# Four transformer layers on one core: the first attention's small matmuls on other array tiles and PSUM banks, and part of the first gated unit on GpSimd

## The chip, the cores and the metric

One core of a Trainium2 chip runs the whole program. The metric is the device time of one execution in microseconds (us), as the median of several runs. TensorE (PE in the profile) multiplies matrices, VectorE (DVE), ScalarE (ACT) and GpSimd (POOL) work elementwise, SyncE (SP) issues most DMAs. Matmuls write to PSUM, which has 8 banks of 512 fp32 columns by 128 partitions.

## The reference, cut to what matters

The input `x` is 16 sequences of 64 rows with 512 columns, handled as 8 row tiles of 128 rows. The program runs four layers of cross attention and feed-forward network. Only the first layer is touched:

```
x = x + attention0(layernorm(x), ctx)     # windows of 16 queries, 32 keys, 8 heads in the 64-row axis
x = x + ffn0(layernorm(x))
# ffn0:
xs = bf16(x); qg, sg = quant(xs * inv_gate); qu, su = quant(xs * inv_up)     # integers up to 127, a scale per row
gate = qg @ w_gate.T * sg * s_wgate
up   = qu @ w_up.T   * su * s_wup
inter = bf16(clip(silu(gate) * up, -10, 10))
qi, si = quant(inter * inv_inter)
out = qi @ w_down.T * si * s_wdown
```

Layers 1 to 3 follow (the second attention with 32 heads of 128 is by far the longest) and are the same code before and after.

## The kernel before, in words

Each engine has its own instruction stream, written in the order of one common list, `ORDER`, which `stage_order` makes; every entry is a stage name and an index. An engine runs its stream in order and waits on semaphores. A stage's PSUM bank comes from `psum_uses`; `psum_table` counts how often each bank is filled, and whoever fills a bank next waits until the last reader has freed it. A bank that two kinds of stage share is therefore handed over in the order of the list.

The first attention is worked in 32 groups `u`, four per row tile. The stages of a group, several steps of the list apart, are:

- `l0_qk` (once in four groups): the projections q and k; ScalarE spreads them out of banks 4 and 7 (L1774, L1780).
- `l0_project` (L795): the values. 16 matmuls with 64 contraction rows, 32 stationary and 128 moving columns. An fp32 matmul shows as two instructions in the trace.
- `l0_scores` (L813 the band mask, L817 the products): four array tiles of 32 by 32, 8 products of 64 columns on each; one bank, 0 and 1 in turn. VectorE takes the maximum and subtracts it (L1372, L1377; the latter frees the bank), ScalarE exponentiates.
- `l0_sum` (L1381, L1384) on VectorE, then GpSimd multiplies (L2158).
- `l0_turn` (L828) transposes, `l0_weigh` (L844) weights the values, `l0_out` (L859) projects into bank 6; VectorE adds that to `X` and frees bank 6 (L1392).

The first ffn of a row tile is interleaved, a stage every half step: layer norm; `f0_quant` and `f0_quant_u` (VectorE L1294 to L1298, ScalarE L1817); the transposes `f0_turn` (bank 7) and `f0_turn_u` (both L750), copied by ScalarE to `qgT`, `quT` (L1836); `f0_gate` on TensorE (L880, L882) and VectorE (L1417, L1418); the exponential on ScalarE (L1850); `f0_silu`; `f0_quant2`; `f0_turn2`; `f0_down` (L896 to L900, bank 6), read by VectorE at L1443. `f0_turn_u` stands in the list directly behind the `l0_weigh` that follows `f0_turn`, so that on TensorE the order there is `f0_turn`, `l0_out`, `l0_weigh`, `f0_turn_u`, `l0_turn`, `f0_gate`. For row tiles 0 to 5 it fills bank 0.

Four groups make one period, which also carries one row tile of ffn. Below its groups are called A, B, C, D: A follows `f0_down`, B holds the two transposes and `f0_gate`, C holds `l0_qk` and `f0_silu`, D holds `f0_quant2`, `f0_turn2` and ends with the next `f0_down`.

Of the kernel before, what the change touches and what calls it, by code (L numbers as in the profile page):

```python
# [17 lines left out]
NT = 8  # L18
# [215 lines left out]
def psum_uses(stage, i):  # L234
# [7 lines left out]
    if stage == "l0_scores":  # L242
        return [("S", (0, 1))]
# [8 lines left out]
    if stage == "f0_turn_u":  # L252
        return [("u", (0 if i < NT - 2 else 3 if i < NT - 1 else 6,))]
# [144 lines left out]
def build_program(nc, d, out):  # L398
    ctx = ExitStack()
    with ctx:  # L400
# [51 lines left out]
        def bank(use):  # L452
            return banks[use.bank // 2][:, 512 * (use.bank % 2):512 * (use.bank % 2) + 512]

# [275 lines left out]
        def tensor_program(pe):  # L730
# [50 lines left out]
            def l0_project(u):  # L781
                t, g = divmod(u, 4)
                cn, d_cn, n_cn = cn_place(t)
                on.wait_ge(D.w0, 16)
                on.wait_ge(D.pad, 16)
                p = PSUM["l0_project", u, "v"]
                on.wait_ge(d_cn, n_cn)
                on.wait_ge(S.zero, 2)
                on.wait_ge(p.free, p.n)
                for k in range(4):  # L790
# [12 lines left out]
            def l0_scores(u):  # L803
                t, g = divmod(u, 4)
                p, q, k = PSUM["l0_scores", u, "S"], PSUM["l0_qk", 4 * t, "q"], PSUM["l0_qk", 4 * t, "k"]
# [4 lines left out]
                pairs = [slice(32 * h, 32 * h + 32) for h in range(4)]  # L810
# [20 lines left out]
            def l0_weigh(u):  # L831
# [8 lines left out]
                for j in range(4):  # L840
                    for p, r in zip((p0, p1), halves):
                        for h in range(4):
                            c = j * 128 + 32 * h
# [59 lines left out]
            def l1_q(i):  # L903
                h, t = divmod(i, NT)
                p = PSUM["l1_q", i, "p"]
                lt_ready("l1", t)
                on.wait_ge(p.free, p.n)
# [83 lines left out]
            def l1_d(i):  # L991
                n = weight_turn(i)
                if n is not None:
                    on.wait_ge(S.mx4, n + 1)
                    on.wait_ge(S.zero, 9)
# [255 lines left out]
        def vector_program(v):  # L1251
# [92 lines left out]
            def begin(_):  # L1344
# [6 lines left out]
                v.memset(mgp, MAGIC).then_inc(S.zero, 1)  # L1351

# [15 lines left out]
            def l0_scores(u):  # L1368
                p = PSUM["l0_scores", u, "S"]
                s3, p3 = [x.rearrange("p (g k) -> p g k", k=32) for x in (em[u % 3], bank(p))]  # L1370
                on.wait_ge(p.full, p.n + 1)
                on.mark(v.tensor_reduce(mx0[u % 2], p3, AX, MAX))  # L1372
# [4 lines left out]
                v.tensor_tensor(s3, p3, bc(mx0[u % 2], 32), SUB).then_inc(p.free, 1)  # L1377
# [31 lines left out]
            def f0_gate(t):  # L1409
# [3 lines left out]
                on.wait_ge(S.sx, t)  # L1413
                if t:
# [5 lines left out]
            def f0_silu(t):  # L1420
                p = PSUM["f0_gate", t, "p"]
# [697 lines left out]
        def pool_program(g):  # L2119
# [54 lines left out]

            def f0_silu(t):
                on.wait_ge(S.it, t + 1)
                if t:
# [103 lines left out]
            def f3_mm(t):  # L2281
# [8 lines left out]
                      f0_silu=f0_silu, f0_down=f0_down, l1_k=l1_k, l1_z=l1_z, f1_quant=f1_quant, l2_begin=l2_begin, l2_a=l2_a, l2_z=l2_z, f2_split=f2_split,  # L2290
# [8 lines left out]
        def sync_program(s):  # L2299
# [14 lines left out]
            def begin(_):  # L2314
# [12 lines left out]
                for c in range(4):  # L2327
                    for k in range(2):
                        load(view(cT, c * 2048 + 192 * k, [[256, 8], [1, 64]]), d["cT"][:, c, k], D.ct)
                load(wq1, d["w1"][0][:, 0:2048], D.wq1)  # L2330
                load(w1, d["w1"][0][:, 2048:3072], D.kv1)

            def l0_norm(u):
# [7 lines left out]
                load_cn(t + 1)  # L2341

# [148 lines left out]
def host_layout(i):  # L2491
# [15 lines left out]
    order = np.arange(128).reshape(2, 8, 8).transpose(1, 0, 2).reshape(128)  # L2507
    p = np.arange(128)
    bq, bk, bv, bo = [np.tile(i[f"L0_xattn_b{n}"], 2)[:, None] for n in "qkvo"]
    pairs = (p[:, None] // 16 % 2 == np.arange(2)[None, :]).astype(np.float32)  # L2510
    own = (p[:, None] // 8 % 2 == np.arange(2)[None, :]).astype(np.float32)
# [74 lines left out]
```

## Time and profile before

| | us |
|---|---|
| median of 3 runs | 1567.65 (1567.29 to 1570.88) |
| profiled execution, its own time | 1568.3 |
| its span, first to last instruction | 1566.5 |
| TensorE busy | 1489.1 (95%) |
| VectorE busy | 819.6 (52%) |
| ScalarE busy | 748.8 (48%) |
| GpSimd busy | 439.2 (28%) |

The granted TensorE clock averaged 0.988 of full speed. Shares over the whole span are means over stages with different limits; the first layer is the first 240 us or so. Times in the trace are counted from the start of the span.

### The profile page before, as it was taken

How to read it: one execution, taken by the hardware profiler on the slowest of the kernel's cores; microseconds unless marked ns; L12 is line 12 of the kernel's file. 1: busy time of each engine (PE TensorE's matmuls, PEld its weight loads, DVE VectorE, ACT ScalarE, POOL GpSimd, SP SyncE). 2: the span in 40 equal slices, each digit the busy share in tenths (PEclk: the TensorE clock that was granted, in tenths of full speed). 3: DMA queues.
4: the chain of work that ended last, by engine and by line, in shares of the span. 5: the costliest groups of instructions: out<-in, count | busy, mean ns of one | idle time of the engine just before them, and what ended most of it. 6: DMA issues, size and time to landing. Idle time of an engine off the chain costs nothing. (4 is left out here: it accounts for less than half of the span.)

```text
span 1566.5 us, 32999 instructions
## 1 busy us (share of the span) xinstructions
PE 1489.1 (95%) x13154; PEld 1228.5 (78%) x13154; DVE 819.6 (52%) x1681; ACT 748.8 (48%) x2560; POOL 439.2 (28%) x557
## 2 busy tenths in 40 slices
PE   6988979999999999999999999879999999999998
PEld 4767768888989888888989887556656778888876
DVE  3678875544444555544443447766665421343465
ACT  4565545454545445454544565355443312455552
POOL 1355343222222212222222224255221000123333
PEclk8999999999999999999999999899999999999999
DMA  8000010020100101010010110020100001122111
GB/s 252 13 17 10 10 44 28 28 75 28 41 28 3 40 27 41 28 41 28 4 38 28 41 55 1 2 83 1 41 1 1 26 6 56 48 74 74 47 27 62
DMA packets 44537, 58.62 MB, mean 37 GB/s; under 512 B 25520, under 2 KB 32704, under 8 KB 41568
## 3 DMA queue, kind: packets, MB, share of 16 engines
q1 hardware_dynamic: 43872, 56.05, 11.4%
q8 instruction: 104, 1.70, 0.5%
q10 hardware_dynamic: 448, 0.46, 0.1%
q14 instruction: 49, 0.40, 0.1%
q0 software_dynamic: 64, 0.00, 0.0%
HBM read 48.89 MB, written 2.10 MB: 33 GB/s over the span
## 5 line engine op out<-in xcount | busy, mean ns | idle before, releaser
L1872 ACT ACTIVATE big<-pb 128x128 f32<-128x128 f32 x384 | 106.5, 277 | 300.9 <-PE pb L912 198.2
L2211 POOL TENSOR_TENSOR big<-big 128x512 f32<-128x512 f32 x96 | 99.9, 1040 | 260.4 <-DVE big L1503 260.4
L1921 ACT ACTIVATE big<-pb,big 128x128 f32<-128x128 f32 x384 | 135.7, 367 | 58.0 <-issue 34.2
L1498 DVE TENSOR_REDUCE big<-pb 128x4 f32<-128x512 f32 x96 | 65.8, 686 | 178.1 <-PE pb L951 170.5
L927 PE MATMUL pb<-wkh,CXh 128*128 128x256 f32 x512 | 150.0, 293 | 0.0
L927 PE MATMUL pb<-wkl,CXh 128*128 128x256 f32 x512 | 145.4, 284 | 0.0
L927 PE MATMUL pb<-wkh,CXl 128*128 128x256 f32 x512 | 144.6, 282 | 0.0
L2201 POOL TENSOR_SCALAR big<-big 128x6 f32<-128x6 f32 x64 | 12.8, 199 | 413.1 <-ACT big L1872 412.5
L1290 DVE TENSOR_TENSOR X<-X,pb 128x512 f32<-128x512 f32 x128 | 86.9, 679 | 74.8 <-PE pb L1138 39.3
L978 PE MATMUL pb<-woh,oh 128*128 128x512 f32 x256 | 114.3, 446 | 0.0
L912 PE MATMUL pb<-wqh,CXh 128*128 128x512 f32 x256 | 101.9, 398 | 3.0 <-DVE big L1468 1.5
L978 PE MATMUL pb<-woh,ol 128*128 128x512 f32 x256 | 103.1, 403 | 0.0
L978 PE MATMUL pb<-wol,oh 128*128 128x512 f32 x256 | 102.0, 399 | 0.0
L912 PE MATMUL pb<-wqh,CXl 128*128 128x512 f32 x256 | 101.3, 396 | 0.0
L912 PE MATMUL pb<-wql,CXh 128*128 128x512 f32 x256 | 101.2, 395 | 0.0
L966 PE MATMUL pb<-big 128*128 128x256 f32 (+1 forms) x384 | 98.8, 380 | 0.1
L927 PEld LDWEIGHTS pb<-wkh,CXl 128*128 128x128 f32 x512 | 97.8, 191 | 0.0
L927 PEld LDWEIGHTS pb<-wkh,CXh 128*128 128x128 f32 x512 | 97.5, 190 | 0.0
L927 PEld LDWEIGHTS pb<-wkl,CXh 128*128 128x128 f32 x512 | 97.4, 190 | 0.0
L1488 DVE COPY big<-pb 128x512 f32<-128x512 f32 x56 | 38.7, 690 | 101.5 <-PE pb L939 101.0
L2128 POOL TENSOR_SCALAR ve<-mv 128x1 f32<-128x1 f32 x64 | 14.3, 224 | 274.7 <-DVE mv L1272 272.6
L2206 POOL TENSOR_TENSOR big<-big,half 128x6 f32<-128x6 f32 x64 | 84.7, 1324 | 9.4
(279 smaller groups left out, 3790.7 us busy)
## 6 DMA issues: line engine op xcount, KB each, us to landing
big<-in_w SPq DMA_DIRECT2D x17, 1024.0 KB, 5.0
big<-in_w SPq DMA_DIRECT2D x24, 256.0 KB, 3.0
big<-in_w SPq DMA_DIRECT2D x8, 512.0 KB, 3.6
o<-o SPq DMA_DIRECT2D x96, 32.0 KB, 1.9
X<-in_x SPq DMA_DIRECT2D x8, 256.0 KB, 5.4
big<-in_cn SPq DMA_DIRECT2D x8, 256.0 KB, 2.8
CXlf<-in_cT SPq DMA_DIRECT2D x8, 256.0 KB, 5.9
big<-in_wa SPq DMA_DIRECT2D x1, 2048.0 KB, 7.6
```

Of the source, the lines that this page charges most:

```text
L912: a = pe.matmul(bank(p), x_rows(x, c, t), y[:, 512 * c:512 * c + 512], start=(n == 0), stop=(n == 11))
L927: a = pe.matmul(bank(p)[:, s * 256:s * 256 + 256], kv_rows(x, c, 2 * t + s), y[:, 256 * c:256 * c + 256], start=(n == 0), stop=(n == 11), ...
L966: a = pe.matmul(bank(p)[0:hd, s * 256:s * 256 + 256], v_of(s), pt[:, s * 256:s * 256 + 256], start=(s == 0), stop=True, skip_group_check=True)
L978: a = pe.matmul(bank(p), x[:, 128 * c:128 * c + 128], y[:, 512 * c:512 * c + 512], start=(n == 0), stop=(n == 3 * size - 1))
L1290: v.tensor_tensor(X[:, t, :], X[:, t, :], bank(p), ADD).then_inc(p.free, 1)
L1488: v.tensor_copy(QT[i % 2].rearrange("p (b h q) -> p h b q", b=2, h=4), bank(p).rearrange("p (h b q) -> p h b q", h=4, b=2)).then_inc(p.fre ...
L1498: v.tensor_reduce(m[j % 2], quarters(bank(p)), AX, MAX, negate=True).then_inc(S.m, 1)
L1872: y = a.activation(sq[i % 2], bank(p)[:, j * width:j * width + 128], ACT.Square, accum_out=ss[i % 2][:, first + j:first + j + 1])
L1921: y = a.activation(e_[:, c], bank(p)[:, c], ACT.Exp, bias=m[j % 2][:, k:k + 1], scale=1.0, accum_out=z[j % 2][:, k:k + 1])
L2128: g.tensor_scalar(ve[:, n % 4, :], mv[:, n % 4, 1:2], 1e-5, None, ADD).then_inc(*on.to(S.pool))
L2206: g.tensor_tensor(rr[i % 2][:, 0:6], ss[i % 2][:, 0:6], half[:, 0:6], ALU.pow).then_inc(*on.to(S.rr))
L2211: g.tensor_tensor(quarters(e_), quarters(e_), bc(r[j % 2], 128), MUL).then_inc(*on.to(S.pn))
```

## The change: tiles, banks, one silu on GpSimd, and later loads

- Values: 64 moving columns in place of 128 per matmul (head channels are laid out so that each batch half needs only its own 64); the other half of the bank is zeroed once, by VectorE, at the start.
- Scores: eight array tiles instead of four, row group h with column groups h and h+2; the first 256 columns of bank 0 and of bank 1 together hold one group. There is one such buffer, so the next group's scores wait until this group's are subtracted.
- `f0_turn_u` of row tiles 0 to 5 goes to bank 6 in place of bank 0.
- `f0_silu`: VectorE keeps the addition of 1 and the reciprocal; GpSimd makes gate times up (early), the product with the reciprocal, and the clamp.
- DMAs of `cT` (8) and of layer 1's weights (2) leave the start of SP's queue and stand behind its loads of `cn` for row tiles 2 and 3.

```diff
     if stage == "l0_scores":
-        return [("S", (0, 1))]
+        return [("S", (1,))]
...
     if stage == "f0_turn_u":
-        return [("u", (0 if i < NT - 2 else 3 if i < NT - 1 else 6,))]
+        return [("u", (6 if i < NT - 2 else 3 if i < NT - 1 else 6,))]
...
-                            a = pe.matmul(bank(p)[key, k * 128:k * 128 + 128], cn[rows_, at:at + 32], wv0[rows_],
-                                          start=(k == 0), stop=True, skip_group_check=True)
+                            a = pe.matmul(view(bank(p)[key], k * 128 + 16 * b, [[32, 4], [1, 16]]), cn[rows_, at:at + 32],
+                                          view(wv0[rows_], 16 * b, [[32, 4], [1, 16]]), start=(k == 0), stop=True,
+                                          skip_group_check=True)
...
-                for r in pairs:
+                tiles = [(e, slice(32 * h, 32 * h + 32), slice((32 * h + 64 * e) % 128, (32 * h + 64 * e) % 128 + 32))
+                         for e in range(2) for h in range(4)]
+                for e, r, c in tiles:
                     b = bandb[r.start:r.start + 16]
-                    pe.matmul(bank(p)[r], b[:, 0:32], b[:, 128:640], start=True, stop=False, skip_group_check=True)
-                for i in range(8):
-                    n = 8 * g + i
-                    for r in pairs:
-                        a = pe.matmul(bank(p)[r, i * 64:i * 64 + 64], Qx[t % 2][r, n * 32:n * 32 + 32],
+                    pe.matmul(two_banks[c, e, 0:256], b[:, 0:32], b[:, 128:384], start=True, stop=False, skip_group_check=True)
+                for i in range(4):
+                    for e, r, c in tiles:
+                        n = 8 * g + 4 * e + i
+                        a = pe.matmul(two_banks[c, e, i * 64:i * 64 + 64], Qx[t % 2][r, n * 32:n * 32 + 32],
...
+                v.memset(bank(PSUM["l0_project", 0, "v"]), 0.0).then_inc(S.zero, 1)
...
                 on.mark(v.tensor_scalar(e0, e0, 1.0, None, ADD))
                 on.wait_ge(S.dve, on.n)
-                on.mark(v.reciprocal(e0, e0))
-                on.wait_ge(S.dve, on.n)
-                on.mark(v.tensor_tensor(e0, e0, g0, MUL))
-                on.wait_ge(S.dve, on.n)
-                on.wait_ge(p.free, p.n + 1)
-                on.mark(v.tensor_tensor(e0, e0, u0, MUL))
-                on.wait_ge(S.dve, on.n)
-                on.wait_ge(S.mi, t)
-                v.tensor_scalar(it0, e0, -10.0, 10.0, MAX, MIN).then_inc(S.it, 1)
+                v.reciprocal(e0, e0).then_inc(S.it, 1)
...
+            def f0_gate(t):
+                p = PSUM["f0_gate", t, "p"]
+                on.wait_ge(S.sg, t + 1)
+                on.wait_ge(p.free, p.n + 1)
+                on.wait_ge(*on.last)
+                g.tensor_tensor(u0, u0, g0, MUL).then_inc(*on.to(S.pool))
+
             def f0_silu(t):
                 on.wait_ge(S.it, t + 1)
+                on.wait_ge(*on.last)
+                g.tensor_tensor(e0, e0, u0, MUL).then_inc(*on.to(S.pool))
+                on.wait_ge(*on.last)
+                g.tensor_scalar(it0, e0, -10.0, 10.0, MAX, MIN).then_inc(*on.to(S.pool))
...
-                for c in range(4):
-                    for k in range(2):
-                        load(view(cT, c * 2048 + 192 * k, [[256, 8], [1, 64]]), d["cT"][:, c, k], D.ct)
-                load(wq1, d["w1"][0][:, 0:2048], D.wq1)
-                load(w1, d["w1"][0][:, 2048:3072], D.kv1)
...
                 load_cn(t + 1)
+                if t == 1:
+                    for c in range(4):
+                        for k in range(2):
+                            load(view(cT, c * 2048 + 192 * k, [[256, 8], [1, 64]]), d["cT"][:, c, k], D.ct)
+                if t == 2:
+                    load(wq1, d["w1"][0][:, 0:2048], D.wq1)
+                    load(w1, d["w1"][0][:, 2048:3072], D.kv1)
```

The order of the stages is the same. TensorE's stream in a group B, before (pb3 holds banks 6 and 7, pb0 banks 0 and 1; a wait on `bank6_free` is for VectorE's L1392):

```order
L795 MATMUL pb1<-big 32x128 x15
L750 MATMUL pb3<-ident,big 128x128 [waits f0_q_gate]
L750 MATMUL pb3<-ident,big 128x128 x3
L859 MATMUL pb3<-big 128x128 [waits bank6_free,bank5_free,bank4_free]
L859 MATMUL pb3<-big 128x128
L844 MATMUL pb2<-big 32x32 [waits bank3_free]
L844 MATMUL pb2<-big 32x32 x31
L750 MATMUL pb0<-ident,big 128x128 [waits bank0_free,f0_q_up]
L750 MATMUL pb0<-ident,big 128x128 x3
L828 MATMUL pb1<-ident,big 128x128 [waits l0_probs]
```

The same place after the change (its line numbers are a few higher: L752 for L750, L866 for L859, L835 for L828):

```order
L798 MATMUL pb1<-big 32x4x16 x15
L752 MATMUL pb3<-ident,big 128x128 [waits f0_q_gate]
L752 MATMUL pb3<-ident,big 128x128 x3
L866 MATMUL pb3<-big 128x128 [waits bank6_free,bank5_free,bank4_free]
L866 MATMUL pb3<-big 128x128
L851 MATMUL pb2<-big 32x32 [waits bank3_free]
L851 MATMUL pb2<-big 32x32 x31
L752 MATMUL pb3<-ident,big 128x128 [waits bank6_free,f0_q_up]
L752 MATMUL pb3<-ident,big 128x128 x3
L835 MATMUL pb1<-ident,big 128x128 [waits l0_probs]
```

No row has moved; the second transpose waits for bank 6, which the `l0_out` two rows above it fills, where it waited for bank 0.

VectorE's stream in the same group B after the change, from the layer norm statistics of the next row tile to the read of that `l0_out`; it is the same sequence as before:

```order
L1385 TENSOR_REDUCE big<-pb0 128x16 [waits bank1_full]
L1390 TENSOR_TENSOR big<-pb0,big 128x512 [waits dve_step,bank3_full]
L1278 BN_STATS st<-X 128x6 [waits d_row4]
L1282 BN_AGGR mv<-st 128x2 [waits dve_step,ln_rows]
L1296 TENSOR_SCALAR xn<-X,mv,rs 128x512 [waits bank4_full,ln_rstd]
L1405 SCALAR_TENSOR_TENSOR X<-pb3,big,X 128x128 [waits bank6_full]
```

L1405 (L1392 before) is what frees bank 6, and it stands behind the group's own scores, the statistics and the normalized rows.

## Rows read from the trace of the kernel before

**Rows 1.** Windows: stretch, length, busy PE, PEld, DVE, ACT, POOL (instructions), clock, DMA share, GB/s.
```profile
0.00:88.26 88.26, 70.53 (x2017) 52.33 (x2018) 46.72 (x106) 46.75 (x93) 22.14 (x35) 0.94 0.41 120
88.26:197.42 109.16, 97.87 (x2930) 77.79 (x2930) 86.91 (x188) 64.29 (x135) 54.98 (x64) 1.00 0.04 11
144.22:170.82 26.60, 23.99 (x733) 19.31 (x732) 21.57 (x47) 15.10 (x32) 11.41 (x15) 1.00 0.05 14
197.42:243.18 45.76, 36.55 (x900) 31.28 (x899) 31.66 (x67) 22.11 (x56) 16.92 (x19) 0.93 0.12 38
243.18:1566.50 1323.32, 1284.13 (x7314) 1067.08 (x7312) 654.33 (x1320) 615.63 (x2276) 345.15 (x440) 0.99 0.11 34
```

**Rows 2.** Timeline of TensorE, one period: start, duration, engine, line, instruction, idle before.
```profile
144.22 0.39 PE L813 MATMUL pb<-big 16*32 16x512 bf16 x4
144.44 1.06 PE L817 MATMUL pb<-big 32*32 32x64 f32 x64
145.44 1.08 PE L795 MATMUL pb<-big 64*32 64x128 f32 x32
146.44 0.71 PE L859 MATMUL pb<-big 128*128 128x128 f32 x4
...
148.36 0.39 PE L813 MATMUL pb<-big 16*32 16x512 bf16 x4
...
150.59 0.66 PE L750 MATMUL pb<-ident,big 128*128 128x128 f32 x4
...
151.62 0.76 PE L844 MATMUL pb<-big 64*32 64x32 f32 x64
...
152.79 0.65 PE L750 MATMUL pb<-ident,big 128*128 128x128 f32 x4 [0.42 <-ACT big L1817]
...
155.05 0.39 PE L880 MATMUL pb<-CXh,qgT 128*128 128x256 f32 x1 [1.17 <-ACT qgT L1836]
...
157.57 0.40 PE L813 MATMUL pb<-big 16*32 16x512 bf16 x4
```

**Rows 3.** Timeline of ScalarE, VectorE and GpSimd in that period.
```profile
144.33 0.75 DVE L1443 SCALAR_TENSOR_TENSOR big<-pb,big 128x512 f32<-128x512 f32 x1 [1.17 <-PE pb L900]
...
149.13 0.82 ACT L1817 ACTIVATE big<-big 128x512 f32<-128x512 f32 x1 [0.92 <-DVE big L1298]
...
155.60 0.35 DVE L1392 SCALAR_TENSOR_TENSOR X<-pb,big,X 128x128 f32<-128x128 f32 x1
...
158.69 0.69 DVE L1310 TENSOR_TENSOR CXl<-pb,CXh 128x512 fp32r<-128x512 f32 x1 [0.56 <-ACT CXh L1721]
...
159.29 0.68 DVE L1372 TENSOR_REDUCE big<-pb 128x16 f32<-128x512 f32 x1
...
161.01 1.75 DVE L1425 RECIPROCAL big<-big 128x256 f32<-128x256 f32 x1
...
162.79 0.42 DVE L1427 TENSOR_TENSOR big<-big 128x256 f32<-128x256 f32 x1
...
163.71 0.29 DVE L1433 TENSOR_SCALAR big<-big 128x256 bf16<-128x256 f32 x1
...
164.09 0.68 POOL L2181 TENSOR_TENSOR big<-big 128x256 f32<-128x256 bf16 x1 [6.13 <-DVE big L1433]
...
165.07 0.36 DVE L1294 TENSOR_REDUCE big<-big 128x1 f32<-128x256 f32 x1
...
165.23 1.05 POOL L2158 TENSOR_TENSOR big<-big 128x512 f32<-128x512 f32 x1 [0.47 <-DVE big L1384]
```

**Rows 4.** Windows around two stretches in which TensorE stood still, columns as in Rows 1.
```profile
30.74:33.92 3.18, 0.00 (x1) 0.00 (x0) 0.00 (x0) 0.14 (x1) 0.00 (x0) 0.98 0.60 131
33.92:40.40 6.48, 6.48 (x123) 4.72 (x127) 3.55 (x7) 3.00 (x7) 0.00 (x0) 0.50 0.80 286
231.10:233.88 2.78, 0.01 (x2) 0.03 (x1) 1.32 (x6) 1.27 (x4) 2.30 (x4) 1.00 0.85 330
233.88:238.80 4.92, 4.92 (x29) 4.92 (x30) 1.41 (x4) 3.09 (x11) 0.00 (x0) 0.65 0.03 10
```

More of the change, by code:

```diff
@@ L453, in bank @@
             return banks[use.bank // 2][:, 512 * (use.bank % 2):512 * (use.bank % 2) + 512]
+        two_banks = banks[0].rearrange("p (e n) -> p e n", e=2)
         X = sb("X", [128, NT, 512])
@@ L789, in l0_project @@
                 on.wait_ge(p.free, p.n)
+                on.wait_ge(S.zero, 9)
                 for k in range(4):
@@ L804, in l0_scores @@
                 t, g = divmod(u, 4)
-                p, q, k = PSUM["l0_scores", u, "S"], PSUM["l0_qk", 4 * t, "q"], PSUM["l0_qk", 4 * t, "k"]
+                q, k = PSUM["l0_qk", 4 * t, "q"], PSUM["l0_qk", 4 * t, "k"]
+                p = PSUM["l0_scores", u, "S"]
                 on.wait_ge(q.free, q.n + 1)
@@ L842, in l0_weigh @@
                         for h in range(4):
-                            c = j * 128 + 32 * h
+                            c = j * 128 + 32 * ((h + j // 2 * 2) % 4)
                             a = pe.matmul(bank(p)[32 * h:32 * h + 32, j * 32:j * 32 + 32],
@@ L906, in l1_q @@
                 lt_ready("l1", t)
+                if i == 0:
+                    scores = PSUM["l0_scores", 4 * NT - 1, "S"]
+                    on.wait_ge(scores.free, scores.n + 1)
                 on.wait_ge(p.free, p.n)
@@ L994, in l1_d @@
                     on.wait_ge(S.mx4, n + 1)
-                    on.wait_ge(S.zero, 9)
+                    on.wait_ge(S.zero, 10)
                     turn_b(PSUM["l1_d", i, "w4"], q4[n % 2])
@@ L1369, in l0_scores @@
                 p = PSUM["l0_scores", u, "S"]
-                s3, p3 = [x.rearrange("p (g k) -> p g k", k=32) for x in (em[u % 3], bank(p))]
+                s4 = em[u % 3].rearrange("p (e g k) -> p e g k", e=2, k=32)
+                p4 = two_banks[:, :, 0:256].rearrange("p e (g k) -> p e g k", k=32)
+                m3 = mx0[u % 2].rearrange("p (e g) -> p e g", e=2)
                 on.wait_ge(p.full, p.n + 1)
-                on.mark(v.tensor_reduce(mx0[u % 2], p3, AX, MAX))
+                on.mark(v.tensor_reduce(m3, p4, AX, MAX))
                 if u >= 3:
@@ L1376, in l0_scores @@
                 on.wait_ge(S.dve, on.n)
-                v.tensor_tensor(s3, p3, bc(mx0[u % 2], 32), SUB).then_inc(p.free, 1)
+                v.tensor_tensor(s4, p4, m3.unsqueeze(3).broadcast_to([128, 2, 8, 32]), SUB).then_inc(p.free, 1)
             def l0_sum(u):
@@ L1413, in f0_gate @@
                 on.wait_ge(S.sx, t)
+                on.wait_ge(S.mi, t)
                 if t:
@@ L1420, in f0_silu @@
             def f0_silu(t):
-                p = PSUM["f0_gate", t, "p"]
                 on.wait_ge(S.sx, t + 1)
@@ L2289, in pool_program @@
             do = dict(begin=begin, l0_bias=l0_bias, l0_norm=l0_norm, l0_sum=l0_sum, l0_ctx=l0_ctx, f0_norm=f0_norm,
-                      f0_silu=f0_silu, f0_down=f0_down, l1_k=l1_k, l1_z=l1_z, f1_quant=f1_quant, l2_begin=l2_begin, l2_a=l2_a, l2_z=l2_z, f2_split=f2_split,
+                      f0_gate=f0_gate, f0_silu=f0_silu, f0_down=f0_down, l1_k=l1_k, l1_z=l1_z, f1_quant=f1_quant, l2_begin=l2_begin, l2_a=l2_a, l2_z=l2_z, f2_split=f2_split,
                       l3_z=l3_z, l3_c=l3_c, f3_mm=f3_mm)
@@ L2505, in diag @@
         return z
-    order = np.arange(128).reshape(2, 8, 8).transpose(1, 0, 2).reshape(128)
+    order = np.arange(128).reshape(2, 4, 16).transpose(1, 0, 2).reshape(128)
     p = np.arange(128)
     bq, bk, bv, bo = [np.tile(i[f"L0_xattn_b{n}"], 2)[:, None] for n in "qkvo"]
-    pairs = (p[:, None] // 16 % 2 == np.arange(2)[None, :]).astype(np.float32)
-    own = (p[:, None] // 8 % 2 == np.arange(2)[None, :]).astype(np.float32)
+    pairs = (p[:, None] // 8 % 2 == np.arange(2)[None, :]).astype(np.float32)
+    own = (p[:, None] // 16 % 2 == np.arange(2)[None, :]).astype(np.float32)
     m["w0"] = np.concatenate([diag(i["L0_xattn_Wq"].T)[:, order], diag(i["L0_xattn_Wk"].T)[:, order],
```

1 line of the change is left out of this document (removed).

## The prediction, made before the changed kernel ran

> **What bounds the kernel now.** I read the busy shares first: TensorE is busy 95% of the span. That is a mean, and the change touches only the first layer, so I read the windows by stage next [rows 1]. From 243 us on the stream is as before, and TensorE is busy 1284 of 1323 us there, so whatever shift stands at 243 us stands at the end. In the first layer one period of four groups lasts 26.60 us, with TensorE busy 23.99 and VectorE 21.57 [rows 1]: TensorE leads, VectorE is close behind. Third came the timelines of that period, to see which engine each wait ends on [rows 2, 3]. VectorE starts L1443 at 144.33, right behind the down projection, and from there to the end of L1392 at 155.95 it is never free for long: 11.62 us of work in a row, the GpSimd steps of two layer norms included [rows 3]. TensorE does not wait for that L1392 before; it only matters that the bank is free a group later.
>
> **The matmuls.** In a group, scores take 144.22 to 145.44, or 1.22 us, values 145.44 to 146.44, or 1.00 us [rows 2]. The scores' 64 instructions of 64 columns on four tiles run at 1.06/64 = 16.6 ns each. The value matmuls also occupy only four different tiles (two row halves, two column groups for each) and now have 64 columns, so I price them like the scores: 32 x 16.6 ns = 0.53 us, a gain of 0.47. Bounds: 32 instructions at the 11.9 ns of L844 (0.76/64, eight tiles [rows 2]) give 0.38; no gain gives 1.00. Scores on eight tiles: from 64 x 11.9 ns = 0.76 less what the modelled end adds, to the present 1.06 us; I take 0.69, as L844 is the only row with eight tiles and its successor starts sooner than its end. The masks (0.22 us) I leave as they are. Together 0.84 us less per group, 32 groups, or 27 us, if TensorE were always the bound.
>
> The Trainium skill, page "TensorE: Matmul & The Clock Gate", section "Part 1: The HAM clock gate", says that the start-to-start distance of matmuls never falls under about 25 ns, however few columns they have. L844's 64 instructions in 0.76 us [rows 2] contradict it for tiled matmuls, and so do the scores. By the page the values would gain 0.2 us per group instead of 0.47 and the scores nothing; the first 88 us would then give back about 4 us less.
>
> **The wait that is added.** In group B the second ffn transpose (L750 at 152.79) now needs bank 6, which the l0_out just before it has filled and which only VectorE's L1392 frees. In this period that ends at 155.95 [rows 3]. I place everything from the end of the down projection, 144.22. TensorE's new arrival: group A's 4.14 us less 0.84, scores and values of B 1.22 + 1.00 - 0.84, that is 148.90; it waits for ScalarE's L1817 (149.13 + 0.82) until 150.0; transpose, l0_out, l0_weigh as in 150.59 to about 152.3, so it stands at the transpose at 151.7. VectorE's 11.62 us have not become shorter: nothing in them waits for TensorE, and none of their instructions is removed. So TensorE idles from 151.7 to 156.0, 4.3 us, where it lost 0.42 before. Behind the transpose in its queue are l0_turn, the gate matmuls, and group C. Transpose and l0_turn take 1.1 us, so the gate starts at 157.1 where it started at 155.05 (before, it waited 1.17 us for ScalarE's quantized rows [rows 2], which are now ready early): 2.0 us late.
>
> From there to the next down projection the chain doesn't run over TensorE's scores. VectorE's L1372 of group C starts behind L1310 at 159.29 [rows 3], after the scores are done; then the reciprocal, sum, quant2, scores of D, ScalarE's copy of the quantized rows, transpose, down projection. It took 170.82 - 157.57 = 13.25 us. The silu part: before, the reciprocal ends at 162.76, two products and the clamp go on to 163.92, GpSimd's product (0.68) ends at 164.77, 2.0 us in all. Now GpSimd does product, clamp, product. I take 0.65 for a 256-column fp32 product (between VectorE's 0.42 and the 0.68 of L2181, whose one operand is bf16; half of L2158's 1.05 is 0.53), 0.5 for the clamp (between VectorE's 0.29 and 0.68), 0.68, and 0.2 of handing over: 2.0 us again. VectorE sheds 1.13 us per row tile there, but l0_out's addition and l0_sum take only 1.15, and then quant2 (L1294) waits for GpSimd about 0.9 us: it starts 2.3 us behind the reciprocal, at 165.05, against 165.07. So the 9 us taken from VectorE over eight row tiles buy at most 0.2 per period. Bounds: clamp and product at 0.4 together gain 0.2 (then group D's scores on TensorE are last), at 1.6 they cost 0.5.
>
> Sum of a period at full clock: 11.7 to the freed bank, 3.7 to group C's scores (transpose and l0_turn 1.1, gate and l1_turn 2.5), 13.0 from there: 28.4 us against 26.6. The four periods of 88.26:197.42 took 109.16 us, two of them longer through casts and instruction stalls that partly hide in the new idle; new 4 x 28.4 + 0.5 = 114.1, so +4.9. A fifth such wait follows in 197.42:243.18 (row tile 5; tiles 6 and 7 keep their banks); I take it like the others, 1.8, less 0.3 for its faster scores: +1.5.
>
> **The clock.** Where TensorE stood still for 3.18 us, the granted clock was 0.50 for the next 6.48 us; after 2.78 us it was 0.65 over 4.92 us [rows 4]. 0.50 and below-one means are time at the lower of its two levels, 1.2 GHz. Losses: 6.48 x 0.50 = 3.2 us and 4.92 x 0.35 = 1.7 us. After the 1.17 us before L880 it stayed at full speed. The new stillness of 4.3 us is longer than both, and what follows it (gate, l1_turn, scores of C) is on the path. I charge 2.0 us each, five times: +10. Bounds 0 and 3.2 each.
>
> **The first 88 us.** Nine groups have no wait on bank 6. Light groups gain the full 0.84. Those with l0_qk gain only about 0.4, because l0_weigh then waits for ScalarE's spreading of q, which starts from VectorE's subtraction. Groups around the first gate gain little, since VectorE leads. Added up: u0 0.6, u1 0.3, u2 0.4, u3 1.3 (it runs at half clock), u4 and u5 0.85 each, u6 0.2, u7 0.85, u8 0.4, u10 and u11 0.5 together: 6.3 us. The single score buffer costs nothing where VectorE is ready: its two reads take at most 1.72 us (159.29 to 161.01 [rows 3]), while TensorE has 148.36 - 145.44 - 0.47 = 2.45 us of other work between two scores [rows 2]. The moved loads: TensorE stood still 3.18 us at 30.74 while DMA was 60% busy [rows 4]; cT is now issued from about 25 on, so the same collision can come again. I count 1 us for them, bounds 0 and 6 (stall and clock gone).
>
> **Sum.** -6.3 - 1 + 4.9 + 1.5 + 10 = +9.1, on the profiled execution: span 1575.6, own time 1577.4 with the 1.8 us around it. The median of the runs lay 0.65 below that execution: 1576.8, say 1577.
>
> **Rivals.**
> - The clock doesn't fall, or what it costs is hidden behind VectorE: +9.1 - 10 = -0.9, 1567. For it: much of C waits on ScalarE anyway. Against it: two stretches in the trace, both shorter. Chance 0.17; within 0.3%.
> - The long fall: 3.2 us each and GpSimd at its upper bound, +6 and +2.5: 1585. Chance 0.15.
> - Faster: the loads decide. The stall at 30.74 and its slow stretch go (-5 more), tiles reach their lower bounds (-2), and the clock's price is 1 us each or less (-5): 9.1 - 12 = -3, 1565; it decides once the clock costs under 1.2 us each and the stall is gone. If in addition VectorE's chain up to L1392 shortens by 2 us, so that the wait is hidden (it would need another engine's step in it to go, and I see none), the five waits vanish: 1552. Chance together 0.15, of which 0.12 faster by over 0.3%.
>
> My forecast has 0.53. Changes within 0.3% (4.7 us) can't be told from none here. Slower by more: the forecast and the long fall, nearly all, 0.67; within: 0.20; faster: 0.13. Range: 1564 to 1586.
>
> **What would show it.** In the new profile: the second transpose of five groups B with about 4 us idle before it, released by VectorE's read of l0_out; a granted clock of 0.5 to 0.7 behind each; periods of 29 to 31 us; value matmuls of 0.5 us per 32; L1294's 256-column form with an idle of 0.5 to 1 us ended by GpSimd; VectorE's idle before the gate up by 2 us. Wrong would be: periods under 27 us, which means VectorE reaches that L1392 sooner than 11.6 us after the down projection; no idle before the transpose; value matmuls still 1 us.

## The result, and the profile after

The median of the changed kernel is 1591.66 us (4 runs, 1587.02 to 1592.70), that of the kernel before in the same job 1567.47 (4 runs, 1563.49 to 1570.88). The ratio is 1.015, 95% interval 1.0118 to 1.0181: slower by 24 us, where +9 was forecast. The direction was right, the time lies outside the range. The profiled execution took 1592.56 us against 1568.3, so the traces differ by the same 24 us. They are compared stage by stage below; each is one execution, and a stage of one execution can be off by several us, as shown further down. One of the six executions of e11 (below) was a slow run, 1865.71 us at a granted clock of 0.743, and neither its ratio nor its median in the table uses it.

The page of the changed kernel: span, busy time and share of each engine, and the granted clock in 40 slices of about 40 us.
```profile
span 1590.5 us, 33255 instructions
PE 1478.3 (93%) x13282; PEld 1223.0 (77%) x13282; DVE 810.6 (51%) x1658; ACT 750.1 (47%) x2560; POOL 460.9 (29%) x581
PEclk7899879999999999999999999999999999999999
```
TensorE is busy 11 us less than before and the kernel takes 24 us more, so its waiting grew by 35. The matmuls alone are about 24 us shorter at full clock (0.75 us in each of 32 groups, below); the busy time fell by less than half of that, because more of it ran at the low clock. The low digits stand in the first seven slices, the first layer.

Windows of the changed kernel, cut at the same places of the program as [rows 1] (scores of groups 12, 20, 28, and the same matmul of the second attention's stream at 268.57):
```profile
0.00:91.45 91.45, 65.02 (x2064) 48.79 (x2065) 46.04 (x104) 46.94 (x93) 24.76 (x38) 0.85 0.40 116
91.45:218.42 126.97, 96.49 (x2993) 79.63 (x2992) 81.64 (x176) 64.85 (x135) 65.30 (x76) 0.88 0.03 10
122.78:153.95 31.17, 23.48 (x749) 19.34 (x748) 20.45 (x44) 16.87 (x35) 18.71 (x21) 0.89 0.04 12
218.42:268.57 50.15, 34.56 (x915) 30.04 (x915) 30.58 (x64) 22.03 (x56) 19.51 (x22) 0.86 0.11 34
268.57:1590.50 1321.93, 1282.25 (x7314) 1064.52 (x7312) 652.32 (x1314) 616.33 (x2276) 351.35 (x446) 0.99 0.11 34
```
Against [rows 1]:

| stretch | before | after | difference | in the prediction |
|---|---|---|---|---|
| up to group 12 | 88.26 | 91.45 | +3.2 | -7.3 |
| four periods | 109.16 | 126.97 | +17.8 | +12.9 (4.9 and four clock falls) |
| to the common point | 45.76 | 50.15 | +4.4 | +3.5 (1.5 and a fifth fall) |
| the rest | 1323.32 | 1321.93 | -1.4 | 0 |
| sum | | | +24.0 | +9.1 |

TensorE in one period after, to be laid beside [rows 2]:
```profile
122.91 0.84 PE L824 MATMUL pb<-big 32*32 32x64 f32 x64
123.67 0.65 PE L798 MATMUL pb<-big 64*32 64x64 f32 x32
124.25 0.71 PE L866 MATMUL pb<-big 128*128 128x128 f32 x4
...
130.25 0.76 PE L851 MATMUL pb<-big 64*32 64x32 f32 x64
134.85 1.09 PE L752 MATMUL pb<-ident,big 128*128 128x128 f32 x4 [3.84 <-DVE X L1405]
135.73 1.06 PE L835 MATMUL pb<-ident,big 128*128 128x128 f32 x4
136.44 0.56 PE L887 MATMUL pb<-CXh,qgT 128*128 128x256 f32 x1
136.80 0.42 PE L889 MATMUL pb<-wgl,qgT 128*128 128x256 f32 x1
...
140.38 0.30 PE L820 MATMUL pb<-big 16*32 16x256 bf16 x8
...
153.95 0.30 PE L820 MATMUL pb<-big 16*32 16x256 bf16 x8
```
From start to start the scores take 0.76 us (1.00 before), the values 0.58 (1.00 before), the masks 0.13 (0.22 before): 0.75 us less per group, where the prediction had 0.84. Then the second transpose stands 3.84 us for VectorE's L1405, the read that frees bank 6, and what follows runs slowly: behind the first pair, the gate's matmuls (L887 and L889 in turn) start 0.21 us apart, where at full speed they start 0.12 apart. The windows of that place, with the clock in the third column from the right:
```profile
131.01:134.85 3.84, 0.00 (x1) 0.03 (x1) 2.64 (x7) 3.00 (x7) 1.75 (x3) 0.74 0.01 4
134.85:140.47 5.62, 5.62 (x36) 5.46 (x44) 1.12 (x4) 1.27 (x2) 2.33 (x2) 0.57 0.00 0
140.47:153.95 13.48, 10.70 (x368) 8.06 (x366) 9.30 (x20) 9.00 (x19) 7.39 (x9) 1.00 0.08 24
```
The clock falls within this standstill already (0.74 over it). 5.62 us at a mean clock of 0.57 (86% of it at 1.2 GHz) are 5.62 x 0.43 = 2.4 us lost, on the path to group C.

This happens six times, once for each row tile 0 to 5: the waits at the second transpose are 1.03, 3.85, 3.84, 2.70, 4.11 and 5.44 us, and the clocks from there to the next group's masks 0.62, 0.53, 0.57, 0.65, 0.55 and 0.63. Worked out the same way, an estimate, the six slow stretches lose 12.9 us together.

VectorE and GpSimd in that period, beside [rows 3]:
```profile
122.89 0.75 DVE L1448 SCALAR_TENSOR_TENSOR big<-pb,big 128x512 f32<-128x512 f32 x1 [1.45 <-PE pb L907]
...
134.36 0.34 DVE L1405 SCALAR_TENSOR_TENSOR X<-pb,big,X 128x128 f32<-128x128 f32 x1
...
140.05 0.48 DVE L1431 SCALAR_TENSOR_TENSOR big<-pb,big 128x256 f32<-128x256 f32 x1 [4.47 <-PE pb L889]
...
145.65 0.73 POOL L2190 TENSOR_TENSOR big<-big 128x256 f32<-128x256 f32 x1 [3.85 <-DVE big L1438]
146.46 1.08 POOL L2192 TENSOR_SCALAR big<-big 128x256 bf16<-128x256 f32 x1
147.69 0.68 POOL L2197 TENSOR_TENSOR big<-big 128x256 f32<-128x256 bf16 x1
...
148.41 0.42 DVE L1304 TENSOR_REDUCE big<-big 128x1 f32<-128x256 f32 x1 [1.78 <-POOL big L2197]
```
From L1448 to the end of L1405 are 11.8 us (11.6 before): VectorE's chain is what it was, and TensorE, which now comes to it earlier, waits for it. VectorE in turn waits 4.47 us for the gate, where it waited 0.41 before:
```profile
157.24 0.48 DVE L1417 SCALAR_TENSOR_TENSOR big<-pb,big 128x256 f32<-128x256 f32 x1 [0.41 <-PE pb L882]
```
GpSimd's clamp takes 1.08 us.

### The profile page after: what moved, and what is told of

Same layout as the page of the kernel before. It is cut to its first block and busy times, and to the rows that moved or that the text cites. A ratio compares the mean times of both kernels' runs of the same rounds, so it can differ in the third digit from the quotient of the medians.

```text
span 1590.5 us, 33255 instructions
## 1 busy us (share of the span) xinstructions
PE 1478.3 (93%) x13282; PEld 1223.0 (77%) x13282; DVE 810.6 (51%) x1658; ACT 750.1 (47%) x2560; POOL 460.9 (29%) x581
## 5 line engine op out<-in xcount | busy, mean ns | idle before, releaser
L1503 DVE TENSOR_REDUCE big<-pb 128x4 f32<-128x512 f32 x96 | 65.9, 686 | 178.6 <-PE pb L961 170.2
L2217 POOL TENSOR_SCALAR big<-big 128x6 f32<-128x6 f32 x64 | 12.9, 202 | 410.4 <-ACT big L1877 409.7
```

Source lines behind the costliest of these rows:

```text
L1503: v.tensor_reduce(m[j % 2], quarters(bank(p)), AX, MAX, negate=True).then_inc(S.m, 1)
```

## The experiments

Fifteen kernels ran. The ratio is always to the kernel before on the same chip; 0.1% is 1.6 us. "us" is ratio less one, times 1568. Differences between two rows carry both intervals; they are given below as plus or minus so many us.

| kernel | median | ratio (95%) | us |
|---|---|---|---|
| e1 before, transpose in bank 6 | 1584.08 | 1.0092 (1.0071 to 1.0114) | +14.4 |
| e2 after, transpose in bank 2 | 1576.46 | 1.0059 (1.0039 to 1.0079) | +9.3 |
| e3 after, the wait filled | 1580.70 | 1.0073 (1.0048 to 1.0099) | +11.4 |
| e4 before, values alone | 1570.55 | 1.0004 (0.9988 to 1.0020) | +0.6 |
| e5 before, GpSimd silu alone | 1570.43 | 1.0020 (1.0010 to 1.0031) | +3.1 |
| e6 after, silu on VectorE | 1589.37 | 1.0141 (1.0121 to 1.0161) | +22.1 |
| e7 after, `l0_rows` later | 1579.50 | 1.0083 (1.0053 to 1.0113) | +13.0 |
| e8 before, `l0_rows` later | 1568.95 | 1.0009 (0.9996 to 1.0022) | +1.4 |
| e9 before, moved loads alone | 1568.76 | 1.0007 (0.9996 to 1.0018) | +1.1 |
| e10 before, scores alone, transpose in bank 2 | 1571.71 | 1.0036 (1.0018 to 1.0053) | +5.6 |
| e11 after, loads early | 1591.44 | 1.0155 (1.0132 to 1.0177) | +24.3 |
| e12 before, four matmuls added | 1565.92 | 0.9994 (0.9984 to 1.0004) | -0.9 |
| e13 before, transpose in bank 2 | 1569.46 | 1.0003 (0.9990 to 1.0016) | +0.5 |
| e14 before, bank 6, wait filled | 1578.24 | 1.0066 (1.0052 to 1.0080) | +10.3 |
| e15 after, bank 3, silu on VectorE | 1585.42 | 1.0108 (1.0087 to 1.0128) | +16.9 |

### The bank: e1, e2, e15, e13

e1, the kernel before with one number of the table of banks:
```diff
-        return [("u", (0 if i < NT - 2 else 3 if i < NT - 1 else 6,))]
+        return [("u", (6 if i < NT - 2 else 3 if i < NT - 1 else 6,))]
```


> The kernel before, with one edit: f0_turn_u of row tiles 0 to 5 fills bank 6 in place of bank 0. Theory W (the wait on bank 6 and the clock behind it are the whole of the slowdown in the periods): the second transpose waits for VectorE's L1392, 3.2 us later than it ran, the gate starts 2.0 us later, five times, and the clock falls behind each; +10 us for the waits and +8 to +15 for the clock, so 1586 to 1593. Rival M (the slowdown comes from the new matmul shapes, the single score buffer, GpSimd's silu or the moved loads): under +6 us.

Measured +14.4 us: a little under what W forecast, far over M. None of the new matmuls and none of GpSimd's new steps is in this kernel, so 14 of the 24 us come from one number. Its four periods:
```profile
86.16:208.50 122.34, 103.95 (x2929) 85.17 (x2928) 86.81 (x188) 64.85 (x135) 55.02 (x64) 0.92 0.03 10
```
That is 30.6 us a period against 27.3. The prediction had 109.16 + 12.9 = 122.1 for the four periods of the changed kernel: right for this kernel, though partly by luck. The sum had 1.2 us a period for the wait and 2.0 for the clock; the section on e14 below finds 1.8 and 1.5.

e2 is the counterpart, the changed kernel with `(2 if i < NT - 2 ...`. Bank 2 holds the values' zeroed halves, which the transpose overwrites, so the attention of later groups differs in value, not in work.

> The kernel after, with one edit: f0_turn_u of row tiles 0 to 5 fills bank 2, which ScalarE's copy of the values frees, in place of bank 6. Theory W: the transpose then runs about 1.5 us earlier, the gate 1.6 us earlier, and the stillness of TensorE before it is under 3 us; each period gives back 1.6 us and the part of the clock's loss that the shorter stillness spares: 1572 to 1582. Rival M: within 4 us of the kernel after.

As expected: 14 of the 24 us are gone (plus or minus 6; 15 by the medians), 9 remain. Its waits at the transpose are 2.1 to 2.75 us in five of six periods, for ScalarE's copy of the values (L1766), so bank 2 is not free of a wait here. e15 put the transpose in bank 3 and the silu part back on VectorE.

> The changed kernel with the second ffn transpose in bank 3 (free as soon as ScalarE has copied the weights turned just before) and with the products and the clamp back on VectorE: what is left of the change are the scores, the values and the loads. Theory (parts add up: after 1592 less 14.4 for bank 6 less 3 for the silu part, less the bank-2 wait of the earlier run): 1570 to 1575, not faster than before, since VectorE leads the periods. Rival (with both brakes gone the faster matmuls show): 1560 to 1566.

Both missed, by 10 us or more. Bank 3 moves the wait one instruction on: `l0_turn`, next in TensorE's queue, needs the same bank, which ScalarE's copy L1850 (L1841 in the changed kernel) must first read.
```profile
131.42 1.09 PE L835 MATMUL pb<-ident,big 128*128 128x128 f32 x4 [2.67 <-ACT quT L1850]
```
A standstill of 2.67 us, and the transposes behind it take 1.09 us and not 0.66. e13, the control for bank 2:

> The kernel before with the second ffn transpose in bank 2 in place of bank 0, nothing else. In the run with the new scores and bank 2 that transpose waited 0.7 to 2.0 us for ScalarE's spreading of the attention rows (the reader of the values' bank). Theory (part of that run's 4 us is this wait and not the scores): 2 to 4 us more than before, 1569 to 1572, with idles of 0.7 to 2 us before the transposes. Rival (the scores themselves): within 1 us of before.

+0.5 us (-1.6 to 2.5), though its trace shows idles of 1.25 to 2.3 us ahead of these transposes. With the old matmuls bank 2 costs nothing that can be measured. e10 below has the new scores and bank 2: the bank alone doesn't explain its cost, but the two together were not tried apart.

### Wait or clock: e3, e14

The transpose stays in bank 6, and four matmuls whose result nothing reads fill the wait:
```diff
             def f0_turn_u(t):
                 on.wait_ge(S.qu, t + 1)
+                if t < NT - 2:
+                    ...
+                    for _ in range(4):
+                        pe.matmul(bank(p3)[:, 0:512], ident[:, :], xu0, start=True, stop=True, ...)
                 turn_ints(PSUM["f0_turn_u", t, "u"], xu0, 4)
```


> The kernel after, with four fp32 matmuls of 512 columns (about 0.9 us each at full clock, results thrown away, into bank 3 before l0_turn overwrites it) in front of each f0_turn_u of row tiles 0 to 5, so that TensorE is busy while it waits for bank 6. The wait itself stays. Theory C (the lower clock behind the wait costs 2 to 3 us per period): 10 to 15 us faster than the kernel after, with a granted clock of 1.0 in the gate matmuls. Rival (the wait alone costs, the clock's loss is hidden behind the other engines): no change, or up to 5 us slower where the fillers outlast the wait.

> The kernel before with the transpose in bank 6 (the run that cost 14 to 16 us) and, ahead of it, four 512-column fp32 matmuls whose result nothing reads, so that TensorE works while it waits. Theory W (of the cost per period about 1.8 us is the wait itself, six of them, and 1 us or more the clock): 1575 to 1580, the clock at 1.00 through most periods. Rival C (nearly all is the clock): 1568 to 1572. Rival N (the clock is hidden behind the other engines): 1582 to 1586, as without them.

e3: work was added and the changed kernel became about 12 us faster (1.0150 to 1.0073, plus or minus 6). e14: 4 us less than e1 (plus or minus 4), in the range of W; N's 1582 to 1586 is missed. The traces show how. First e14, the place where TensorE would have waited, and its four periods:
```profile
131.88 3.70 PE L875 MATMUL pb<-big,ident 128*128 128x512 f32 x8 [0.39 <-ACT big L1824]
135.42 0.60 PE L750 MATMUL pb<-ident,big 128*128 128x128 f32 x4
135.85 0.60 PE L828 MATMUL pb<-ident,big 128*128 128x128 f32 x4
```
```profile
92.21:209.88 117.67, 110.31 (x2961) 83.65 (x2960) 86.92 (x188) 64.44 (x135) 55.03 (x64) 1.00 0.04 10
```
Then e1 at the same place:
```profile
129.99 0.63 PE L750 MATMUL pb<-ident,big 128*128 128x128 f32 x4 [3.04 <-DVE X L1392]
130.46 0.84 PE L828 MATMUL pb<-ident,big 128*128 128x128 f32 x4
130.95 0.56 PE L880 MATMUL pb<-CXh,qgT 128*128 128x256 f32 x1
131.31 0.41 PE L882 MATMUL pb<-wgl,qgT 128*128 128x256 f32 x1
```
The clock is 1.00 over the four periods of e14 and 0.92 in e1. A period lasts 29.4 us in e14. VectorE's read (L1399 there) ends at 135.05 and the transposes start at 135.42; over the four periods they start 0.37 to 0.94 us behind the read, 0.5 on the mean, where the changed kernel has 0.15. So the added matmuls run some 0.35 us over: with the wait alone a period is 29.4 - 0.35 = 29.05, or 1.8 over before. e1 has 30.6, so the clock costs 1.5 there. e3's four periods last 118.64 us, 29.7 each: over those of the changed kernel, 31.7, the clock costs 2.1 to 2.4 there. The medians, over six waits and with the overrun added, give about 1.0 per wait for e14 against e1 and 2.2 for e3 against after.

### VectorE's order: e7, e8

```diff
-    l0 = [("l0_rows", 1), ("l0_out", 7), ("l0_sum", 4), ("l0_ctx", 7), ...
+    l0 = [("l0_out", 7), ("l0_sum", 4), ("l0_ctx", 7), ("l0_rows", 1), ...
```


> The changed kernel with one entry of the stage list moved: VectorE (and all other engines) do l0_rows, the normalized rows of the next unit, behind l0_out, l0_sum and l0_ctx and not ahead of them. VectorE's read that frees bank 6 then comes 1.5 to 2.5 us sooner. Theory (the wait for the bank decides, and the clock falls with the length of that wait): the wait shrinks from 3.8 to about 2 us, so 5 x 1.8 = 9 us less, and 0 to 5 us more where the clock stays up: 1578 to 1584. Rival (what is behind l0_rows now waits instead, the products of the next unit come later for ScalarE and TensorE): no gain, 1588 to 1594.

> The kernel before with the same entry moved (l0_rows behind l0_out, l0_sum and l0_ctx). It has no wait for bank 6, so by the theory nothing is gained there: 1564 to 1572. If VectorE's order counts by itself, the time moves by more than 4 us either way, and the run after with the same move must be read against this one.

Both as the theory said: the same move takes 10 to 12 us (by the ratios, plus or minus 6, and by the medians) from the changed kernel and nothing from the one before. In the four periods the waits at the transpose are 2.07 to 2.28 us in e7. This shows that the order of VectorE's instructions ahead of the read sets a good part of the cost.

### The other parts, each alone: e4, e5, e6, e9, e11, e10

e4 has the value matmuls with 64 columns and the zeroed halves.

> The kernel before with one part of the change: value matmuls of 64 moving columns (with the new channel order and the bank zeroed once). TensorE does 0.42 us less per group. Theory W: this part alone is a gain, half of 32 x 0.42 = 13 us where TensorE is the bound: 5 to 9 us faster. Rival K (less busy TensorE lets the clock fall more often in the first 90 us, which eats the gain): no change, with lower granted clock between 20 and 90 us.

No gain, though 0.4 us of TensorE's work goes in each of 32 groups: rival K's outcome, and its sign too, a granted clock of 0.86 over 20 to 90 us against 0.93 before. e5 and e6 change who does the products:
```diff
-                on.mark(v.reciprocal(e0, e0))
-                on.mark(v.tensor_tensor(e0, e0, g0, MUL))
-                on.mark(v.tensor_tensor(e0, e0, u0, MUL))
-                v.tensor_scalar(it0, e0, -10.0, 10.0, MAX, MIN).then_inc(S.it, 1)
+                v.reciprocal(e0, e0).then_inc(S.it, 1)      # the rest on GpSimd, as after
```


> The kernel before, with GpSimd's products and clamp of the gated unit alone. Theory (the wait for bank 6 and the clock behind it make nearly all of the loss; the silu part is neutral): within 2 us of before, since what VectorE sheds per row tile (three instructions, 1.2 us) it spends waiting for GpSimd, whose clamp took 1.08 us in the profile after and not 0.5. Rival S (the silu part itself costs, because the down projection of each tile comes later): GpSimd's three steps and the clamp add 1.7 to 2.5 us to the chain from the reciprocal to the integers, of which the two instructions of l0_out and l0_sum hide 1.15, so 0.6 to 1.3 us per row tile, 5 to 10 us over eight: 1573 to 1578.

> The changed kernel with the products and the clamp back on VectorE; all else as after. Theory (silu neutral): 1588 to 1592, no gain against after. Rival S: 5 to 10 us less than after, 1582 to 1587, the idle of 1.78 us before the 256-column form of L1304 gone.

e5 also zeroes the values' bank and has the new channel order, as e4 does at +0.6. It costs 3.1 us (1.6 to 4.9), between the two theories; e6 gains 1.4 by the ratios (1.0150 to 1.0141) and 2.3 by the medians, which the runs can't tell from nothing. VectorE of e5 at the place where the theory saw it wait:
```profile
164.93 0.25 DVE L1391 RECIPROCAL big<-big 128x16 f32<-128x16 f32 x1
166.85 0.42 DVE L1300 TENSOR_REDUCE big<-big 128x1 f32<-128x256 f32 x1 [1.67 <-POOL big L2191]
```
The loads:

> The kernel before with the moved loads alone (cT and the first weights of the second block, issued by SyncE behind the second and third ffn's waits and not at the start). Theory (the loads are hidden, since nothing reads them before 200 us; the stretch from 20 to 45 us is as often stalled as before): within 3 us of before. Rival L (in the changed kernel TensorE stood 2.3 to 2.8 us in three places of the first 35 us for nothing that the profile shows, while the DMA share was 0.56 over 20:45; the moved loads are to blame): 3 to 8 us more than before, three such stalls and a granted clock under 0.7 over 20:45.

> The changed kernel with the loads back at the start. Theory (loads hidden): 1588 to 1593. Rival L: 3 to 8 us less than after, with the stalls of the first 35 us gone.

Both show the loads hidden, and rival L fallen: e9 +1.1 us, e11 no faster than after. The scores:
```diff
+                tiles = [(e, slice(32 * h, 32 * h + 32), ...) for e in range(2) for h in range(4)]
-                    for r in pairs:
+                    for e, r, c in tiles:
```


> The kernel before with the scores on eight tiles over two banks and one score buffer alone; values with 128 columns as before, the second ffn transpose in bank 2, so that it waits for no late read. Theory (scores cost 0.30 us less per group; the first 88 us gain up to 2, the periods nothing, for VectorE leads there as well): 1565 to 1570. Rival K (TensorE is less busy and its clock falls more often, as with the 64-column values): 2 to 6 us more than before, 1570 to 1574, the granted clock over 20:90 under that of before.

+5.6 us (2.8 to 8.3), as rival K said, and not the gain that I expected. Its kernel also has the transpose in bank 2, so its control is e13: 5.1 us over that, plus or minus 3.5. Four periods of e10 take 112.96 us at a granted clock of 0.95, those of e13 111.91 at 0.97, those of the kernel before 109.16 at 1.00. Whether the clock, the single buffer or TensorE's own standstills (below) do it was not tried apart, and stays open.

### e12: a miss of its own

> The kernel before with four 512-column fp32 matmuls added, whose result nothing reads, ahead of the last row tile's first ffn transpose, where TensorE stood 2.77 us at 231.1 and ran 4.92 us at a mean granted clock of 0.65 behind. Theory (the fall of the clock follows the stillness and costs what the rows show): the clock stays at 1.00 over 234:239, and the time falls by 1 to 1.7 us, which five rounds can hardly tell from none; 1565 to 1568. Rival (what follows waits for other engines, so the clock costs nothing there): stages at 250 us stand as before.

The added matmuls ran at 278 us: the transposes at 231 are those of the last tile but one, which I had misread. So this kernel is nearly the kernel before, its time is the same within the interval, and it can't answer its question. Its trace answers another. It has the same standstill, and the windows before and behind it are:
```profile
228.32:231.10 2.78, 0.00 (x2) 0.03 (x1) 1.30 (x5) 1.28 (x4) 2.31 (x4) 1.00 0.81 315
231.10:236.02 4.92, 4.92 (x72) 4.80 (x73) 1.41 (x4) 3.63 (x16) 0.00 (x0) 1.00 0.03 12
```
In the kernel before the same 2.78 us were followed by 4.92 us at 0.65 [rows 4]. The same wait is paid for in one execution and not in another.

No version beats the kernel before. The parts, each alone, sum to 14.4 + 0.6 + 3.1 + 1.1 + 5.6 = 24.8 us, plus or minus 6, the 24 of the whole: they add up, and none of them is shown to be a gain. Without bank 6 they sum to 10.4, and e2, the changed kernel with bank 2, has 9.3.

## Why the prediction was right and wrong

**The wait.** Right in place, releaser and length: 3.84 us against 4.3 forecast, VectorE's chain 11.8 us against 11.7. Its price per period, 28.4 - 26.6 = 1.8 us, is what e14 shows. The count was wrong: the sum charges five such waits, and six row tiles use bank 6. I then took 2.3 us off the four periods, since casts and stalls of two of them "partly hide in the new idle". They don't: e14's four periods are 7.1 us longer than before even without the overrun of the added matmuls, against 4.9 in the sum.

**The clock.** Forecast 2.0 us for each wait, measured 1.5 in e1 and 2.1 to 2.4 after. The rival without a fall is refuted by e3 and e14. The slow stretches together lose about 13 us in the trace, near the 12 that e3 gives back, where the sum had 10 for five.

In the period of 122.78 to 153.95 the legs are 12.1 us to the transposes behind the wait, 5.5 to group C's masks and 13.6 from there to the next period; the prediction had 11.7, 3.7 + 2.0 and 13.0. So a period is 0.8 us longer than forecast, most of it behind group C, where GpSimd's part lies. The last of the four periods is the odd one, 34.3 us. There TensorE stands once more, in the middle of a group's 64 score instructions and with no releaser in the trace, and the 7.29 us from there to the period's end run at a clock of 0.53:
```profile
211.13 0.36 PE L824 MATMUL pb<-big 32*32 32x64 f32 x16 [1.60 <-issue]
```
e11, the same but for the loads, stands 1.62 us at the same instruction, keeps a clock of 1.00 behind it, and has 30.0 us for that period and 122.6 for the four, where 122.1 was forecast. So of the 4.9 us between +12.9 and +17.8 some 4 are the course of one execution, and the match with e11 is in part luck: the 2.3 taken off for the hiding were wrong. Where the other runs of the changed kernel, of much the same length, spend their time no trace shows.

**GpSimd.** "2.0 us again" failed. The products were sized well (0.73 against 0.65), the clamp was not: 1.08 us against 0.5, and with the product before it 1.81 us, above my upper bound of 1.6 for the two. VectorE waits 1.78 us for GpSimd and not 0.9. e5 prices the part at 3.1 us over eight row tiles.

**The first 88 us: the step that failed most.** "Added up: u0 0.6, u1 0.3, ... 6.3 us", and 1 for the loads: -7.3 was forecast, +3.2 came, 10.5 of the 15 us that I was wrong by. The loads' gain of 1 us is not there in e9 or e11. Single executions scatter here: of the six profiles with the old scores and values and no wait on bank 6 (before, e5, e8, e9, e12, e13) group 12 starts at 84.3 to 90.2, mean 88.2; of the five with both new ones and bank 6 (after, e3, e6, e7, e11) at 88.5 to 92.9, mean 91.0. Two things failed.

The first is the wait of row tile 0. It stands in group 9, inside this stretch. The prediction says that nine groups have no wait on bank 6, and its list goes from u8 to u10: the wait of u9 was put at nothing without a reason. The second transpose and group 10's masks, before:
```profile
72.41 0.66 PE L750 MATMUL pb<-ident,big 128*128 128x128 f32 x4
...
75.30 0.40 PE L813 MATMUL pb<-big 16*32 16x512 bf16 x4
```
After:
```profile
74.20 0.63 PE L752 MATMUL pb<-ident,big 128*128 128x128 f32 x4 [1.03 <-DVE X L1405]
...
78.64 0.30 PE L820 MATMUL pb<-big 16*32 16x256 bf16 x8
```
4.44 us in place of 2.89, at a clock of 0.62, and the wait before it. From group 8 to group 12 the six old profiles take 26.2 us on the mean and the two with bank 6 added (e1, e14) 28.3; the new matmuls with bank 2 or 3 (e2, e15) take 24.5, with bank 6 (after, e3, e6, e11) 27.3. So this wait costs 2 to 3 us, and the 1.6 us that the matmuls gain here go with it.

The second is the gain itself. Group 8 starts at 58.3 to 63.4 in the eight profiles with the old scores and values, mean 61.8, and at 63.3 to 65.9 in the seven with the new ones, mean 64.4: a loss of 2.6 us ahead of any wait on bank 6, where the sum has a gain of some 5. 2.0 of these 2.6 are there when group 3 starts. Why no gain comes can be seen between 42 and 57 us, where both kernels start and end together. Before:
```profile
42.48 0.71 PE L859 MATMUL pb<-big 128*128 128x128 f32 x4
...
52.82 0.63 DVE L1372 TENSOR_REDUCE big<-pb 128x16 f32<-128x512 f32 x1
...
54.88 0.61 PE L859 MATMUL pb<-big 128*128 128x128 f32 x4
...
56.88 0.75 PE L844 MATMUL pb<-big 64*32 64x32 f32 x64 [1.39 <-ACT big L1774]
57.55 0.66 PE L828 MATMUL pb<-ident,big 128*128 128x128 f32 x4
```
After:
```profile
42.49 1.22 PE L866 MATMUL pb<-big 128*128 128x128 f32 x4
...
52.79 0.63 DVE L1385 TENSOR_REDUCE big<-pb 128x16 f32<-128x512 f32 x1
...
53.91 0.61 PE L866 MATMUL pb<-big 128*128 128x128 f32 x4
56.85 0.75 PE L851 MATMUL pb<-big 64*32 64x32 f32 x64 [2.33 <-ACT big L1779]
57.52 0.96 PE L835 MATMUL pb<-ident,big 128*128 128x128 f32 x4
58.41 0.41 PE L820 MATMUL pb<-big 16*32 16x256 bf16 x8
```
TensorE gains 0.97 us over these groups and spends them before L851. VectorE's L1372 / L1385 starts at the same time in both, for VectorE has its own queue (maxima, sums, the low parts of the weights, which wait for ScalarE's casts), and what ScalarE spreads comes behind it. I had called these groups light because TensorE did not wait in them before; two engines were about level, and only one became faster. And the longer stand, 2.33 us against 1.39, is followed by slow instructions: L835 takes 0.96 us where L828 took 0.66. Over 20 to 45 us the granted clock is 0.59 after and 0.80 before, over 45 to 90 us 0.92 and 1.00. Over 20 to 90 us it is 0.90 to 0.95 in the eight profiles with the old scores and values, 0.86 in e4, 0.87 in e10, and 0.77 to 0.87 in the seven with both new ones. That the lower clock turns no gain into a loss is argued and not shown: no run filled the standstills of this stretch.

**The rivals.** The long fall had the clock at 3.2 us each; its time, 1585, was nearer, but its reason isn't what happened. "Faster by the loads" fell with e9 and e11. That the new scores could cost time by themselves was no rival of mine, and it was one that ought to have stood there: e10 shows it.

Another rival was neither written down nor tested. TensorE's standstills for which the trace names no releaser ("issue") sum over the first 245 us to 11.0 to 15.7 us in the eight profiles with the old scores and values, to 17.8 in e4, 20.4 in e10 and 16.6 to 26.0 in the seven with both new ones (13.4 before, 23.2 after). So where matmuls were shortened there is more such standstill, in part at the same instruction in several kernels. What the engine stands for there, and how much of the 10 us beside bank 6 it makes, stays open.

## What to carry to other kernels

An engine that leads with 90% busy isn't the bound where a second one has 81%: lay the second's queue beside it before counting a gain, group by group. In a pool of banks a transfer's new home is priced by who reads that bank last and what that reader has queued ahead; here one number in a table cost 14 us, and moving one entry of the stage list took some 10 of the changed kernel's 24 back. Count the places where the new wait stands, the first one too. Where TensorE waits, price the wait and the slow stretch behind it apart: filling the wait with matmuls that nothing reads separates them in one run.

## What the runs showed of the hardware

- Added, useless matmuls made a kernel faster: by 12 us, plus or minus 6, with six waits filled (e3 against after), and by 4, plus or minus 4, in e14 against e1.
- The fall of the clock isn't a function of the length of a standstill: 2.78 us were followed by 4.92 us at 0.65 in one execution and at 1.00 in another, and 1.60 us by 7.29 us at 0.53 in the changed kernel, where 1.62 us at the same instruction of e11 were followed by a clock of 1.00.
- GpSimd's two-sided clamp of 128x256 fp32 to bf16 took 1.08 us, longer than its product of two fp32 operands of that size (0.73); on VectorE they took 0.29 and 0.42 [rows 3].
- The 64 scores instructions on eight tiles start over 0.76 us, 11.9 ns each, as L851 with half the columns [rows 2]; on four tiles they took 1.00. The Trainium skill, page "TensorE: Matmul & The Clock Gate", section "Part 1: The HAM clock gate", says that the distance from start to start never drops below about 25 ns, and makes no exception for tiles; on several tiles these rows lie below it, so there the measurement decides.
- Shorter matmuls went with a lower clock and with more standstill that no engine releases: 0.77 to 0.87 against 0.90 to 0.95 over 20 to 90 us, a stretch with one wait on bank 6 at most, and 16.6 to 26.0 us against 11.0 to 15.7 over the first 245.
